# Expert rows that carry residual, gate and token number, and a scatter of each finished slot tile to the output

## The reference, cut to what matters

```python
h = layernorm(x)                                   # 1024 tokens, 256 features
logits = h @ Wr + br                               # 8 experts
idx   = argmax(logits)
gate  = softmax(logits)[idx]
out   = zeros
for e in range(8):
    y = gelu(h @ W1[e] + b1[e]) @ W2[e] + b2[e]    # W1[e] 256 x 1024, W2[e] 1024 x 256
    out += y * (gate * (idx == e))
x = x + out                                        # the result, float32
```

## Time and profile before

| | us |
|---|---|
| median of 3 runs | 884.33 (883.62 to 888.43) |
| the profiled execution | 884.7 |
| its span | 882.7 |
| start of `stage_f` in it | 721.0 |
| its first four BATCH_NORM_STATS2 (line 99, from 721.05) | 1.41 |
| first slot tile, first matmul of line 2125 | 760.85 |
| last matmul (line 2135) ends | 857.80 |
| mean granted TensorE clock | 0.885 of full |

### The profile page before, as it was taken

How to read it: one execution, slowest core, us unless ns; L and a number is a source line. 1 busy time by engine, 2 the same in 40 slices (tenths; PEclk the granted TensorE clock), 3 DMA queues, 4 the chain that set the end, 5 groups by cost and what they waited for, 6 DMA issues and landing times. The chain is left out here.

```text
span 882.7 us, 18261 instructions
## 1 busy us (share of the span) xinstructions
PE 679.4 (77%) x7350; PEld 509.5 (58%) x7350; DVE 461.6 (52%) x926; ACT 331.7 (38%) x879; POOL 128.1 (15%) x161
## 2 busy tenths in 40 slices
PE   3778887788999999957777874459986753499980
PEld 2566665564566666735653431159986643389970
DVE  5437877665345554236874959785666452001111
ACT  1245553353354445415864562002214141134430
POOL 1011112203000000022343040050000202100003
PEclk9789998999999999967998986678998985599995
DMA  6910000005200000031000000000000027771103
GB/s 175 359 37 2 1 1 1 1 14 183 45 1 2 1 1 1 1 97 28 1 3 1 0 0 1 0 2 2 0 2 1 1 74 251 280 262 37 40 33 95
DMA packets 33861, 45.00 MB, mean 51 GB/s; under 512 B 7776, under 2 KB 28768, under 8 KB 33664
## 3 DMA queue, kind: packets, MB, share of 16 engines
q1 hardware_dynamic: 29568, 34.42, 11.9%
q0 software_dynamic: 2064, 7.74, 2.5%
q10 hardware_dynamic: 2160, 1.89, 0.7%
HBM read 36.30 MB, written 7.73 MB: 50 GB/s over the span
## 5 line engine op out<-in xcount | busy, mean ns | idle before, releaser
L392 ACT ACTIVATE a_pr<-a_bank,a_nms 128x160 f32<-128x160 f32 x128 | 49.2, 392 | 59.1 <-DVE a_nms L722 56.6
L858 PE MATMUL a_bank<-ident,a_pr 128*80 128x128 f32 x256 | 41.4, 289 | 25.8 <-DVE a_pt L698 23.3
L2008 ACT ACTIVATE f_hb<-f_bank,cols 128x128 f32<-128x128 f32 x96 | 35.3, 368 | 55.5 <-PE f_bank L2125 50.3
L858 PEld LDWEIGHTS a_bank<-ident,a_pr 128*80 128x80 f32 x256 | 26.0, 124 | 46.4 <-ACT a_pr L392 31.9
L2125 PE MATMUL f_bank<-f_xts,f_w 128*128 x384 | 50.3, 288 | 0.8 <-DVE f_xts L2078 0.8
L2125 PEld LDWEIGHTS f_bank<-f_xts,f_w 128*128 128x128 f32 x384 | 48.9, 203 | 1.7 <-issue 1.2
L628 DVE TENSOR_REDUCE a_negmx<-a_bank 128x2 f32<-128x320 f32 x64 | 30.4, 475 | 33.3 <-PE a_bank L850 33.3
L698 DVE COPY a_pt<-a_bank 80x512 f32<-80x512 f32 x60 | 41.0, 683 | 10.3 <-PE a_bank L858 9.7
L2135 PE MATMUL f_bank<-f_w,f_hb 128*128 128x256 f32 x192 | 44.0, 383 | 0.0
L1603 ACT ACTIVATE xnorm<-e_ps 128x512 f32<-128x512 f32 x20 | 11.9, 597 | 81.3 <-PE e_ps L1834 81.3
L2135 PEld LDWEIGHTS f_bank<-f_w,f_hb 128*128 128x128 f32 x192 | 36.1, 193 | 4.5
(11 more groups left out here) (356 smaller groups left out, 1565.7 us busy)
## 6 DMA issues: line engine op xcount, KB each, us to landing
f_w<-in_f_w SPq DMA_DIRECT2D x16, 1024.0 KB, 9.5
a_ct<-in_ctxt SPq DMA_DIRECT2D x15, 160.0 KB, 4.7
rows<-in_rows SPq DMA_DIRECT2D x1, 2120.0 KB, 10.4
slots_x<-a_zero POOLq DMA_DIRECT2D x1, 1920.0 KB, 8.3
slots_y<-a_zero POOLq DMA_DIRECT2D x1, 1920.0 KB, 12.6
f_xs<-slots_x ACTq DMA_DIRECT2D x13, 128.0 KB, 2.1
slots_y<-f_yb POOLq DMA_DIRECT2D x12, 128.0 KB, 2.0
x<-in_x SPq DMA_DIRECT2D x2, 512.0 KB, 5.0
```

The source lines that it names most:

```text
L392: i = act.activation(pr[:, p, j, k, :], s_bank[j][:, k * KW:(k + 1) * KW], ACT.Exp, bias=nms[:, p, j, k:k + 1], accum_out=rsum[:, p, 2 * j ...
L858: m = pe.transpose(dst[0:HK, (2 * k + a) * P:(2 * k + a + 1) * P], pr[:, p, j, k, a * HK:(a + 1) * HK], c.ident[:, :])
L2008: act.activation(hb[:, m, :], bank[m % 4][:, 0:P], ACT.Gelu, bias=c.col("f_b1", e * FC + m)).then_inc(z["act"], 1)
```

## The change

- A slot row has `WX` = 2 * 256 + 2 = 514 numbers (2056 bytes): the normalised token, the token itself (the residual), the gate, and the token's number as an integer. `xb` holds the rows of the 8 tiles; `xn` is now its first 256 columns. GpSimd copies `c.x` and the numbers (`f_ids`, a new small input) to it, VectorE writes the gate.
- There is one DRAM tensor `slots` in place of two; the fill in the first stage fills it in one DMA, with the number N = 1024 as token number.
- In the tile loop GpSimd (`write` in place of `store`) copies the upper half of `xs` (residual, gate, number) to one of two buffers `xk`, and the number of the present tile to `row`; VectorE multiplies the result with the gate and adds the residual in a second operation; GpSimd scatters `yb` by `row` straight to the output. Rows whose number is N are left out by a bounds check. It waits until that has landed before it goes on.
- ScalarE's load of the next tile waits for GpSimd's copy (`kept`) too.
- The gathers, the last eight operations on `c.x` and `finish` are gone.

The diff, without most declarations:

```diff
@@ -379,11 +380,11 @@
                     pool.tensor_tensor(tv, tv, wm[:, i, :].unsqueeze(2).to_broadcast([P, KC * HA, DA]),
                                        ALU.add).then_inc(U["wcent"], 1)
                 spread(b)
-            pool.memset(zero[:, :], 0.0).then_inc(W["zero"], 1)
-            pool.wait_ge(W["zero"], 1)
-            for slots in (c.slots_x, c.slots_y):
-                pool.dma_start(slots[0:MAXT * P, :].rearrange("(p a r) d -> p a (r d)", a=MAXT // 3, r=3),
-                               zero[:, :].unsqueeze(1).to_broadcast([P, MAXT // 3, 3 * D])).then_inc(W["cleared"], 16)
+            pool.memset(zero[:, 0:WX - 1], 0.0).then_inc(W["zero"], 1)
+            pool.memset(zero[:, WX - 1:WX].bitcast(U32), N).then_inc(W["zero"], 1)
+            pool.wait_ge(W["zero"], 2)
+            pool.dma_start(c.slots[:, :].rearrange("(p a) d -> p a d", a=MAXT + 1),
+                           zero[:, :].unsqueeze(1).to_broadcast([P, MAXT + 1, WX])).then_inc(W["cleared"], 16)
             pool.wait_ge(T["ot"], B)
             pool.memset(c.dv[:, :, :, :], 0.0).then_inc(W["zero"], 1)
...
@@ -1922,21 +1923,23 @@
+        xs = sb("xs", [P, WX])
+        xk = sb("xk", [P, 2, D + 2])
+        row = sb("row", [P, 1], U32)
+        ids = sb("ids", [P, NT], U32)
...
@@ -1957,6 +1960,7 @@
             sp.dma_start(before[:, :], c.d["before"]).then_inc(z["small"], 16)
             sp.dma_start(ones[:, :], c.d["ones"]).then_inc(z["small"], 16)
             sp.dma_start(tab[:, :], c.d["f_tab"]).then_inc(z["small"], 16)
+            sp.dma_start(ids[:, :], c.d["f_ids"]).then_inc(z["ids"], 16)
 
             for e in range(E):
                 if e > 1:
@@ -1968,25 +1972,36 @@
 
         @block.gpsimd
         def _(pool):
-            pool.memset(zero[:, :], 0.0).then_inc(z["zero"], 1)
-            pool.wait_ge(z["zero"], 1)
-            pool.dma_start(slots_x[MAXT * P:(MAXT + 1) * P, :], zero[:, :]).then_inc(z["stored"], 16)
-            pool.wait_ge(z["stored"], 16)
+            for t in range(NT):
+                pool.tensor_copy(xb[:, t, D:2 * D], c.x[:, t, :]).then_inc(z["xcopy"], 1)
+            pool.wait_ge(z["ids"], 16)
+            pool.tensor_copy(xb[:, :, WX - 1:WX].bitcast(U32).rearrange("p t n -> p (t n)"), ids[:, :]).then_inc(z["xcopy"], 1)
+            pool.wait_ge(z["xcopy"], NT + 1)
+            pool.wait_ge(z["rse"], 1)
             pool.wait_ge(z["posi"], 1)
             for t in range(NT):
-                pool.indirect_dma_start(slots_x, bass.IndirectOffsetOnAxis(ap=posi[:, t:t + 1], axis=0),
-                                        xn[:, t, :], None).then_inc(z["scattered"], 16)
-
-            def store(e, i):
+                pool.indirect_dma_start(slots, bass.IndirectOffsetOnAxis(ap=posi[:, t:t + 1], axis=0),
+                                        xb[:, t, :], None).then_inc(z["scattered"], 16)
+            pool.wait_ge(z["xs"], 16)
+            pool.tensor_copy(xk[:, 0, :], xs[:, D:WX]).then_inc(z["kept"], 1)
+
+            def write(e, i):
+                pool.wait_ge(z["xs"], i * 16 + 32)
+                pool.nop(nofuse=True)
+                pool.tensor_copy(xk[:, bass.ds((i + 1) % 2, 1), :].rearrange("p b n -> p (b n)"), xs[:, D:WX]).then_inc(z["kept"], 1)
+                pool.wait_ge(z["kept"], i + 1)
+                pool.nop(nofuse=True)
+                pool.tensor_copy(row[:, :], xk[:, bass.ds(i % 2, 1), D + 1:D + 2].bitcast(U32).rearrange("p b n -> p (b n)")
+                                 ).then_inc(z["row"], 1)
+                pool.wait_ge(z["row"], i + 1)
                 pool.wait_ge(z["yb"], i + 2)
                 pool.nop(nofuse=True)
-                pool.dma_start(slots_y[bass.ds(i * P, P), :], yb[:, :]).then_inc(z["stored"], 16)
-            end = tiles(pool, store)
-            pool.wait_ge(z["stored"], end * 16 + 16)
-            pool.nop(nofuse=True)
-            for t in range(NT):
-                pool.indirect_dma_start(yg[:, t, :], None, slots_y,
-                                        bass.IndirectOffsetOnAxis(ap=posi[:, t:t + 1], axis=0)).then_inc(z["gathered"], 16)
+                pool.indirect_dma_start(out, bass.IndirectOffsetOnAxis(ap=row[:, 0:1], axis=0), yb[:, :], None,
+                                        bounds_check=N - 1, oob_is_err=False).then_inc(z["stored"], 16)
+                pool.wait_ge(z["stored"], i * 16 + 16)
+                pool.nop(nofuse=True)
+                pool.sem_inc(z["rows_out"], 1)
+            tiles(pool, write)
 
         @block.scalar
         def _(act):
@@ -1995,14 +2010,16 @@
             act.wait_ge(z["sh"], NT)
             act.activation(ex[:, :, :], sh[:, :, :], ACT.Exp).then_inc(z["ex"], 1)
             act.sem_inc(z["act"], 4)
+            act.sem_inc(z["rows_out"], 1)
 
             act.wait_ge(z["scattered"], 16 * NT)
-            act.dma_start(xs[:, :], slots_x[0:P, :]).then_inc(z["xs"], 16)
+            act.dma_start(xs[:, :], slots[0:P, :]).then_inc(z["xs"], 16)
 
             def hidden(e, i):
                 act.wait_ge(z["xst"], i + 1)
+                act.wait_ge(z["kept"], i + 1)
                 act.nop(nofuse=True)
-                act.dma_start(xs[:, :], slots_x[bass.ds(i * P + P, P), :]).then_inc(z["xs"], 16)
+                act.dma_start(xs[:, :], slots[bass.ds(i * P + P, P), :]).then_inc(z["xs"], 16)
                 for m in range(FC):
                     act.wait_ge(z["hid"], i * FC + (m + 1))
                     act.activation(hb[:, m, :], bank[m % 4][:, 0:P], ACT.Gelu, bias=c.col("f_b1", e * FC + m)
@@ -2036,6 +2053,10 @@
                               ALU.is_equal).then_inc(z["hot"], 1)
 
             dve.memset(run[:, 0, :], 0.0).then_inc(z["run"], 1)
+            dve.wait_ge(z["ex"], 1)
+            dve.reduce_sum(se[:, :], ex[:, :, :], AXX).then_inc(z["se"], 1)
+            dve.wait_ge(z["se"], 1)
+            dve.reciprocal(xb[:, :, 2 * D:2 * D + 1].rearrange("p t n -> p (t n)"), se[:, :]).then_inc(z["rse"], 1)
             dve.wait_ge(z["tot"], 1)
             for t in range(NT):
                 dve.wait_ge(z["run"], t + 1)
@@ -2065,10 +2086,6 @@
             dve.tensor_copy(posi[:, :], pos[:, :]).then_inc(z["posi"], 1)
             dve.tensor_tensor(ends[:, 0:E], first[0:1, :], cnt[0:1, :], ALU.add).then_inc(z["ends"], 1)
             dve.memset(ends[:, E:E + 1], 0).then_inc(z["ends"], 1)
-            dve.wait_ge(z["ex"], 1)
-            dve.reduce_sum(se[:, :], ex[:, :, :], AXX).then_inc(z["se"], 1)
-            dve.wait_ge(z["se"], 1)
-            dve.reciprocal(rse[:, :], se[:, :]).then_inc(z["rse"], 1)
 
             def turned(i, slot):
@@ -2083,14 +2100,15 @@
                 dve.tensor_scalar(xts[:, bass.ds((i + 1) % 2, 1), :, :].rearrange("p b k n -> p (b k n)"), bank[4][:, 0:D],
                                   1.0, None, ALU.mult).then_inc(z["xts"], 1)
                 dve.wait_ge(z["ypr"], i + 1)
-                dve.wait_ge(z["stored"], i * 16 + 16)
-                dve.tensor_tensor(yb[:, :], bank[5][:, 0:D], c.row("f_b2", e * D, D), ALU.add).then_inc(z["yb"], 1)
+                dve.wait_ge(z["rows_out"], i + 1)
+                dve.tensor_tensor(yb[:, :], bank[5][:, 0:D], c.row("f_b2", e * D, D), ALU.add).then_inc(z["yb2"], 1)
+                dve.wait_ge(z["yb2"], i + 1)
+                dve.wait_ge(z["kept"], i + 1)
+                dve.nop(nofuse=True)
+                kept = xk[:, bass.ds(i % 2, 1), :].rearrange("p b n -> p (b n)")
+                dve.scalar_tensor_tensor(yb[:, :], yb[:, :], kept[:, D:D + 1], kept[:, 0:D], ALU.mult, ALU.add
+                                         ).then_inc(z["yb"], 1)
             tiles(dve, out_)
-            dve.wait_ge(z["rse"], 1)
-            dve.wait_ge(z["gathered"], 16 * NT)
-            for t in range(NT):
-                dve.scalar_tensor_tensor(c.x[:, t, :], yg[:, t, :], rse[:, t:t + 1], c.x[:, t, :], ALU.mult,
-                                         ALU.add).then_inc(z["xout"], 1)
 
         @block.tensor
         def _(pe):
...
@@ -2184,16 +2201,7 @@
             c.e_mt = sb_d("e_mt", [P, LEVELS, S])
             stage_d(nc, c)
             stage_e(nc, c)
-        stage_f(nc, c)
-        finish(nc, c, out)
-
-
-def finish(nc, c, out):
-    with nc.semaphore("stored") as stored, nc.Block() as block:
-        @block.sync
-        def _(sp):
-            sp.dma_start(out.rearrange("(t p) d -> p t d", p=P), c.x[:, :, :]).then_inc(stored, 16)
-            sp.wait_ge(stored, 16)
+        stage_f(nc, c, out)
 
 
 def kernel(**inputs):
@@ -2253,6 +2261,7 @@
         "levels": _np.tile(_np.stack(levels, 1), (2, 1, 1)).astype(_np.float32),
         "f_w1": a["L1_ffn_W1"], "f_w2": a["L1_ffn_W2"], "f_wr": a["L1_ffn_Wr"],
         "before": _np.triu(_np.ones((P, P)), 1).astype(_np.float32), "ones": _np.ones((P, P), _np.float32),
+        "f_ids": _np.arange(N, dtype=_np.uint32).reshape(NT, P).T,
         "f_tab": _np.tile(tab.astype(_np.float32), (P, 1)),
     }
```

(30 more changed lines are left out.)

## The result

The kernel after takes 875.84 us (median of 4 runs, 872.94 to 878.62), the kernel before beside it 885.82 (883.62 to 888.43): ratio 0.9886, interval 0.9841 to 0.9931. In a later comparison with more runs it was 873.82 against 886.51, ratio 0.985 (0.9813 to 0.9887). So it is faster, by 10 to 13 us, where 16 were forecast (868 for 884.33); the first median lies just outside the stated range (864 to 875.5).

A forecast was written before the change was run, and what follows sets the result against it. Bound by DMA in the early tiles, TensorE to 857.80, then 24.9 us without matmul; last matmul 2.9 later plus a 5.7 tail gives span 866.4, 16.3 less, so 868 us predicted, range 864 to 875.5.

The forecast's parts named there:

- What the tail held, and that it goes: Behind the last matmul: store of the last tile, eight gathers, eight adds and output write, 24.9 us, are removed.
- What comes in its place: Behind the last matmul: bias add, new VectorE operation, GpSimd start, scatter landing, semaphores and stage end, 5.7 us; 19.2 saved.
- the end of the stage, 1.05, stands in both: From last add to output write's issue in before, 1.05 us; taken as the same closing cost in after.
- Longer rows: Token scatters and slot-tile loads: 2056-byte rows cost 0.35 us per transfer waited for, shift 1.4 by load 2.
- Copies ahead of the scatter: Start of the expert stage: GpSimd's copies of x and token numbers, some 3.5 us, fit its idle time; cost 0.
- The new wait in the first tiles: Load 3 waits for GpSimd's copy behind tile 0's slow scatter, issued at 785.7; shift 2.9 us to the last matmul.
- The wait in undisturbed tiles: Later tiles: load lands 0.9 or 0.3 us before TensorE wants it, period stays 7.25, so 0 added.
- rival C: Tile loop: slack too small, GpSimd's work from landing to copy costs 1 us more; +2 to 3.5, 871; chance 0.12.
- B: Early slot-tile loads: DMA turns go by bytes, so the loads' excess doubles; shift some 9 us, 874; chance 0.12.
- D: Early tiles: TensorE's stall for load 1 leaves its clock at 0.50 one tile longer; 875; chance 0.05.
- E: First tiles: tile 0's scatter lands in 3 us, so the new wait falls away; shift 1.4, 866.5; chance 0.08.
- F: Tile loop: bounds-checked scatter takes longer than 2.40 and sets the period; at 5 us more, 890, slower; chance 0.03.

The follow-up runs named there:

- marker: The kernel after plus a block in which SP loads 32 bytes, to mark the end of the expert stage; 876.73 us (one run).
- close: wait_moved, but ScalarE instead of GpSimd waits for the last scatter's landing; 872.15 us against 887.25 for before, ratio 0.9841.
- after_early: The kernel after, with SP's wait for the scatters ahead of the weights of expert 5 instead of 3; ratio to before 0.986.
- paced: The kernel after, with SP holding the weights of expert e (from 3 on) until slot tile e-2 is loaded; ratio to before 0.9906.
- wait_moved: The kernel after, but GpSimd copies the next residual before waiting for its scatter, and VectorE waits for the landing; 873.12 us, ratio to before 0.9851.
- early: close, with SP's wait for the scatters ahead of the weights of expert 5 instead of 3; ratio to before 0.9839.

## Why the prediction was wrong, step by step

- *What the tail held, and that it goes* (24.9 us): right; no row of it is left.
- *What comes in its place*, 5.7: measured 7.4. The two VectorE operations took 1.31 (1.15 forecast), GpSimd's start 0.85 (0.92), the landing 2.2 (2.4). The term that failed is "the end of the stage, 1.05, stands in both": it was 3.0. The 1.05 were measured behind VectorE's adds, while GpSimd's last instruction of before was the eighth gather at 870.71, seven microseconds ahead of the write; its closing (the DRAIN that was over at 874.7) was covered there. Here GpSimd closes last, and its DRAIN of 1.7 us stands behind the landing: 0.2 + 1.7 + 1.0. `marker` shows that it is the stage's closing, `close` that a part of it can be covered.
- *Longer rows*, +0.35 for each transfer that is waited for: the scatter +0.8 (2.40 to 3.21), load 0 +0.9, load 1 -0.3, load 2 +0.7. Load 2 landed 1.9 us later than in before instead of 1.4; it would have been more, but tile 0's last 16 matmuls with W1 took 2.91 us where they took 3.43 in before, and that was luck. Mechanism right, all but load 1 under-sized. An undisturbed load went from 2.1 to 2.7, not 2.45.
- *Copies ahead of the scatter*, 0: the first scatter started 23.8 instead of 23.6 us after the start of the stage; one VectorE operation beside GpSimd's copies took 0.39 instead of 0.17. 0.2, nearly right (0.38 or 0.39 in seven profiles with the copies, 0.17 in the two of before).
- *The new wait in the first tiles*: right. Load 3 was issued at 64.9 for 64.7 forecast, behind GpSimd's copy, behind a scatter of 6.24 (6.25 forecast). It landed 3.6 and not 2.9 later than in before.
- *The wait in undisturbed tiles*, slack 0.9 or 0.3, so 0: failed by 1.0 us. At a new expert the load was 0.5 us late and TensorE waited. The slack was reckoned with a load of 2.45 (it took 2.7) and 0.6 for the new operation (0.85). This is rival C, at a third of its price; and its size hangs on single late landings: 1.0 in after, where all landed on time, 3.3 in `marker`, whose profile has two late ones, more in `after_early`.
- *The range*: it took the 3 first runs of before as its level. With 884.33 for what later runs put at 886 to 887, and a stage that starts anywhere within 5 us by the clock ahead of it, 2 or 3 us on either side were missing in it.

Together: 0.7 in the first tiles, 1.0 in the later ones, 1.7 behind the last matmul make 3.4, the 16.3 forecast less 12.9 found in the stage. The other 4.5 us, by which the gain of the first two profiles (8.4) falls short of the stage's, are the later start of the stage. Rivals B, D, E and F did not come in the kernel after; D's mechanism did in `paced` and `after_early`.

## What to carry to other kernels

Before an end is re-costed, ask which engine closes last in it: the closing time read behind another engine isn't this one's. A wait for a transfer to *land* should stand behind all that the waiting engine does for others; with 0.3 us of slack it works while landings are on time, and each late one goes straight to TensorE and can go on to its clock. A bulk load that is moved runs beside other transfers: here that gained up to 2.9 us where no load waited for a scatter to land, and lost 2.5 us or more where ScalarE's load did.

## What the runs showed that was not expected

- A scatter of 128 rows of 1 KB lands in 2.1 to 2.5 us, and mostly in 6.1 to 7.0 while weights are being loaded. Once the weights were in, ten of these scatters took 3.0 to 4.4 us, two each in `wait_moved`, `marker`, `close`, `early` and `after_early`; each of the ten had a packet of queue q8 (instructions) beside it, and no other scatter behind the weights took over 2.5. No run varies that packet, so that it is the cause is not shown.
- Rows of 2056 bytes went two to a packet: 640 packets for the eight scatters, where I expected 1152.

```profile
q0 software_dynamic: 640, 2.11, 42.8%
```
- With GpSimd the last engine, closing a stage took 3.0 us where 1.05 were read behind VectorE; the difference is GpSimd's DRAIN. What that waits for, and why it still ends 0.9 us behind the landing in `close`, stays open.
